# The bias of the values is added by VectorE, tile by tile, instead of by GpSimd, four tiles at a time

## What is computed

```
q, k, v = xn Wq' + bq, xn Wk' + bk, xn Wv' + bv
attention = softmax(q k' / 16) v                    # one head of 256 per batch
gates = softmax(xn Wg');  2 experts of 16 per token, their scores scaled to a sum of 1
y = sum over the 2 experts of  score * (silu(xn Gate_e') * (xn Up_e')) Down_e'
ffn = y + sigmoid(xn Wsg') * (silu(xn Ws_gate') * (xn Ws_up')) Ws_down'
```

## Time and profile before

| | us |
|---|---|
| median of 3 executions | 563.72 |
| lowest, highest | 562.06, 564.19 |
| the profiled execution | 562.47 |
| its span, first to last instruction | 560.7 |

### The profile page before, as it was taken

The page is one execution under the profiler, slowest core; times in us unless marked ns, Lnnn a source line. Parts: engine busy times, 40 slices in busy tenths (PEclk is TensorE's granted clock), DMA queues, the critical chain, the costliest instruction groups (busy, mean ns, idle before and its releaser), DMA issues.

```text
span 560.7 us, 9991 instructions
## 1 busy us (share of the span) xinstructions
PE 520.9 (93%) x3469; PEld 473.2 (84%) x3469; DVE 396.4 (71%) x806; ACT 280.4 (50%) x467; POOL 191.4 (34%) x170
## 2 busy tenths in 40 slices
PE   3999998899997899989886999999999999999997
PEld 3888987778887789988876988798989898989897
DVE  5778456998985456454453627899696969697986
ACT  3767764355643255444342544836272727272742
POOL 0001010411005666788885043244142323323410
PEclk9999999999998899999998999999999999999999
DMA  8826254302023455674447471062116111112111
GB/s 314 338 104 243 114 226 179 113 30 85 0 85 95 140 167 161 196 255 146 150 147 127 119 251 37 24 223 61 53 57 206 58 56 49 57 55 69 39 57 57
DMA packets 29888, 69.29 MB, mean 124 GB/s; under 512 B 5008, under 2 KB 9488, under 8 KB 28816
## 3 DMA queue, kind: packets, MB, share of 16 engines
q1 hardware_dynamic: 22496, 49.68, 24.7%
q0 software_dynamic: 6912, 18.88, 12.9%
q10 hardware_dynamic: 432, 0.09, 0.1%
HBM read 41.37 MB, written 27.26 MB: 122 GB/s over the span
## 4 chain that ended last, share of the span: by engine, by line
PE 76%; DVE 10%; another core or an unknown queue 4%; ACT 4%; issue 3%; DMA 1%; POOL 0%; SPq 0%; ACTq 0%; DVEq 0%; POOLq 0%
PE ps L723 47%; PE ps L904 8%; PE ps L729 7%; PE ps L845 6%; PE ps L925 5%; PE ps L806 1%; DVE probs_f L1512 1%; DVE blk_xT L1204 1%; ACT probs_f L1194 1%; DMA stage_gu<-in_shared 1%; ACT blk_xT L1009 1%; PE ps L815 1%; DMA blk_x<-rows,row 1%; DVE acc L1294 1%
## 5 line engine op out<-in xcount | busy, mean ns | idle before, releaser
L710 POOL DMA_INDIRECT rows_y<-ytab,slot x64 | 75.5, 1180 | 136.5 <-DVE acc L1528 120.1
L682 POOL DMA_INDIRECT blk_x<-rows,row x80 | 82.1, 1026 | 70.2 <-DVE row L1399 31.5
L723 PE MATMUL ps<-vv,pT 128*128 128x258 f32 x768 | 96.7, 284 | 0.0
L723 PE MATMUL ps<-xT,shared_w 128*128 128x512 f32 x384 | 94.3, 400 | 1.4 <-DVE sil L1280 1.4
L723 PEld LDWEIGHTS ps<-vv,pT 128*128 128x128 f32 x768 | 94.2, 189 | 0.5
L723 PEld LDWEIGHTS ps<-xT,shared_w 128*128 128x128 f32 x384 | 72.3, 192 | 16.8 <-issue 2.1
L723 PE MATMUL ps<-qT,xbT_hi 128*128 128x512 f32 x256 | 79.5, 392 | 1.0 <-ACT scored_t L1009 0.8
L904 PE MATMUL ps<-expert_w,blk_xT 128*128 x480 | 68.3, 292 | 6.6 <-DVE blk_xT L1204 6.4
L904 PEld LDWEIGHTS ps<-expert_w,blk_xT 128*128 128x128 f32 x480 | 61.1, 193 | 8.8 <-issue 8.4
L723 PEld LDWEIGHTS ps<-qT,xbT_hi 128*128 128x128 f32 x256 | 47.2, 188 | 11.9 <-ACT scored_t L1009 2.0
L668 POOL TENSOR_TENSOR expert_w<-stage_e,expert_w 128x768 fp32r<-128x768 f32 x7 | 13.6, 1941 | 115.2 <-ACT expert_w L1009 115.2
(11 more groups left out here) (159 smaller groups left out, 869.3 us busy)
## 6 DMA issues: line engine op xcount, KB each, us to landing
ytab<-blk_y SPq DMA_DIRECT2D x40, 256.0 KB
keys<-xT SPq DMA_DIRECT2D x8, 1024.0 KB, 5.7
stage_e<-in_experts SPq DMA_DIRECT2D x16, 384.0 KB, 3.1
rows<-xn SPq DMA_DIRECT2D x8, 512.0 KB, 2.6
xbT_hi<-keys SPq DMA_DIRECT2D x8, 512.0 KB
xbT_lo<-keys SPq DMA_DIRECT2D x8, 512.0 KB
out<-acc SPq DMA_DIRECT2D x32, 128.0 KB
acc<-in_x SPq DMA_DIRECT2D x7, 512.0 KB, 8.8
```

Of the source, the lines that this page charges most:

```text
L682: e.indirect_dma_start(out=blk_x[:, q, n, :], out_offset=None, in_=rows, in_offset=bass.IndirectOffsetOnAxis(ap=row[:, 2 * b + n:2 * b + n ...
L710: e.indirect_dma_start(out=rows_y[:, r, k, :], out_offset=None, in_=ytab, in_offset=bass.IndirectOffsetOnAxis(ap=slot[:, k, i:i + 1], axis=0),
L723: ins = e.matmul(dst, stationary(p, k), moving(q, k), start=(n == 0), stop=(n == total - 1))
```

## The change

The eight `bias_in` steps of GpSimd become 32 of VectorE, one tile each. They stand at the end of the loop's steps b = 3 to 34, so that in VectorE's queue `bias_in` b-3 comes behind the remainder of `blk_turn` b+2 and ahead of the product `blk_h` of step b+1. GpSimd keeps only the gathers in this stage. `rows_in` waits for its own tile's addition each time, which is an instruction of the same engine.

```diff
     beside = {5: ("qkv_split", 0), ..., 9: ("mix", 0), 10: ("mix", 1),
-              11: ("mix_bias",), 13: ("keys_load", 0), **{15 + 2 * c: ("bias_in", c) for c in range(NCH)}}
+              11: ("mix_bias",), 13: ("keys_load", 0)}
     for b in range(PAIRS + 2):
...
         if b in beside:
             steps.append(beside[b])
+        if 3 <= b < 3 + TILES:
+            steps.append(("bias_in", b - 3))
...
-                elif kind == "bias_in":                       # in pool_program
-                    c = a[0]
-                    if c == 0:
-                        e.wait_ge(bias_loaded, 16)
-                        e.wait_ge(shared_added, 4 * NCH)
-                    these = acc[:, CT * c:CT * (c + 1), :]
-                    e.tensor_tensor(these, these, bvb[:, :].unsqueeze(1).to_broadcast([P, CT, D]), ALU.add).then_inc(
-                        biased, 1)
...
+                elif kind == "bias_in":                       # in vector_program
+                    i = a[0]
+                    if i == 0:
+                        e.wait_ge(bias_loaded, 16)
+                        e.wait_ge(shared_added, 4 * NCH)
+                    e.tensor_tensor(acc[:, i, :], acc[:, i, :], bvb[:, :], ALU.add).then_inc(biased, 1)
...
                     e.wait_ge(gathered[r], 16 * TOPK * (i // YR + 1))
-                    if i % CT == 0:
-                        e.wait_ge(biased, i // CT + 1)
+                    e.wait_ge(biased, i + 1)
```

## The result

| | before | after |
|---|---|---|
| median, us | 563.0 (4 runs) | 556.48 (4 runs, 555.69 to 557.34) |
| ratio, 95% interval | | 0.9885 (0.9865 to 0.9904) |
| profiled execution, us | 562.47 | 556.99 |
| its span, us | 560.7 | 555.1 |

6.5 us less by the medians, 5.6 us by the two spans; 5.6 us had been forecast. The median lies inside the range, and the gain by the spans is the forecast one, to a tenth by luck, as the account further on shows. That holds for the chip of these runs. On one of the other chips the same change was worth 14.6 us, which only one of the rivals had foreseen; the experiments come to that.

What follows compares the result with a forecast made beforehand. GpSimd's queue of gathers and additions was taken to bound the block stage. 5.9 + 0.9 - 0.5 - 0.7 = 5.6 us gained, so 556.9 us profiled and 558.1 us median; range of 8 in 10: 554.0 to 563.8 us.

Steps and rivals of the forecast that it cites:

- one of the rivals: Block stage: TensorE becomes the bound, 18 pairs at 2.8 us each, 15.5 us gained, 548 us; chance 0.07.
- GpSimd's queue bounds the block stage: Block stage with additions: GpSimd is busy 54.78 of 65.90 us and waits for nobody, despite 34% on the page.
- the difference of two paces: Block stage, 18 pairs: 3.66 us a pair with GpSimd's additions, 3.33 without; 5.9 us gained.
- The low clock and the long stop go (+0.9): TensorE's stop at 293 to 300 us and the half-speed work behind it vanish: 0.9 us gained.
- a full last round comes (-0.5): End of the gathers: the short last round may become a full one of 6.7 us; 0.5 us lost.
- VectorE's additions: 0: VectorE's queue, block stage: 32 additions of 0.34 us counted as 0 on the path; upper bound 5.4 us.
- The cover: VectorE's slack around the remainders, thought to hide an addition; without it one per round is exposed, 16 x 0.34 = 5.4 us.
- Collisions 0.7 us: Block stage: gathers starting inside a VectorE addition are delayed, some 3 of 32, 0.7 us lost; bounds 0 and 13.4 us.
- the fourth rival: Block stage: VectorE's additions wait for gathers, at most 3.4 us of it on the path, 561.5 us; chance 0.04.
- the rule that it was laid beside: Trainium skill: VectorE instructions with two SBUF inputs and GpSimd instructions reading SBUF exclude each other; additions could wait 1.01 us.
- its pace of 3.33 us a pair: Block stage before the additions begin: 10 pairs in 33.29 us, taken as the new kernel's pace for 18 pairs, 59.9 us.
- The rival of the useful breaks: Block stage: additions were stops that freed TensorE's results; without them rounds of eight gathers, gain 0 to 2 us; chance 0.16.

## Why the prediction was right, and where not

1. *GpSimd's queue bounds the block stage, in spite of its 34% of the span.* Right. The 32 additions put back on it cost 12.9 of 14.6 us; on VectorE or left out altogether they make no difference (0.9733, 0.9727). On a chip with rounds the same shows in the kernel with the additions outside the block stage (the stage 6.5 us shorter) and in the one with eight additions on VectorE (0.9885).
2. *The gain is the difference of two paces, 5.9 us.* 5.5 us: the 18 pairs took 60.4 in place of 65.9 us, a round 6.68 us as read off before the additions began. The naive sum, 8 x 2.38 = 19 us, and the pace of TensorE, 15.5, were both rightly passed over for this chip. The picture was neater than the trace: between 205.60 and 222.41 the silus of the kernel before come one by one, 2.5 to 3.8 us apart, and GpSimd's waits in these rounds are 1.1 to 1.8 us, not 1.34 to 1.72. The average pace is the same.
3. *The low clock and the long stop go (+0.9), a full last round comes (-0.5).* Their sum was 0.4; from the silu of pair 32 to the end it was 260.2 us before and 259.9 after. The clock of that part is 1.00 in place of 0.92. What each of the two was worth by itself isn't shown.
4. *VectorE's additions: 0.* Right, and safer than I argued: neither twice as many nor an addition on the run to the first remainder was felt. The cover isn't that run's slack but that a round is set by GpSimd and the release behind it.
5. *Collisions 0.7 us.* Too much. 67 gathers have a median of 1.015 us and a longest one of 1.143. Only two gathers started inside an addition. This was a near thing: 12 of the 32 additions started just 0.02 to 0.03 us behind a gather, and what they would have cost ahead of it no run shows. No addition waited for a gather (0.414 to 0.439 us each), so the fourth rival is out; the rule that it was laid beside speaks of instructions of GpSimd that read SBUF, and that a gather counts as one for its whole length no run shows.
6. *The parts that should not change.* The changed kernel came to the first silu 0.6 us earlier; this is there by 30 us of the span, far ahead of the change, and in other runs of kernels with the same first stage it goes either way (0.2 us later with twice the additions, 1.2 us earlier with eight on VectorE). Between the first silu and that of pair 14 it took 0.8 us more, nearly all of it up to pair 4 (13.87 in place of 13.11 us). There its clock was at the lower level from 187.8 to 194.6 us, 6.8 us in place of the 3.4 of before. That this is the cause is likely, not shown.

The sum of the spans: 5.5 + 0.3 + 0.6 - 0.8 = 5.6 us. That it meets the forecast to a tenth is luck: the pace gave 0.4 us less and the end 0.1 less, the collisions didn't take their 0.7, and the two unforeseen parts took 0.2. The mechanism and the size of the main term were right. By the medians the gain was 6.5 us, and the median came 1.6 us below the 558.1 of the forecast.

What the prediction didn't see is that its pace of 3.33 us a pair belongs to the chip. I used it as it stood and gave TensorE's own pace 0.07. On the chip with 552.2 us that rival holds, 14.6 us where it said 15.5, and 537.65 us lies far below the range. Nothing in one trace could have told that another chip has no rounds; but the words "I can't tell from the trace why; I only use that it repeats" marked the place, and the range stopped at 554.0 us, short of the rival's 548. The rival of the useful breaks is out: without additions GpSimd stopped by itself in every round, for 1.4 to 1.8 us from 202 us on.

## What to carry to other kernels

Look for the bound in a stage, not in the span: an engine of 34% can be a full queue in the stage that counts, and the test is whether it waits for anybody there. Where the same work runs with and without the suspected cost in one trace, the difference of the two paces forecast the gain (5.9 for 5.5 us) far better than the cost that was removed (19 us), on a chip like that of the trace; on another chip the gain was 14.6 us. Before work is moved to where an engine idles, see what its neighbour does there: GpSimd's additions were free for VectorE beside operands in PSUM and made VectorE some 5.8 us late beside operands in SBUF.

## What the runs showed of the hardware

- While GpSimd issues gathers, semaphores are raised late, in batches; TensorE's results so become usable some 0.8 us after a row of gathers ends: 6.68 us for two pairs where TensorE needs 2 x 2.80. Seven raises of TensorE within 0.38 us stand against 2.80 us for the same seven without the effect. The traces of the first result and of the second and third chip show it (kernel before at 562.9 to 563.4 us), the first chip of the experiments does not (552.2 us). Plain DMAs of another queue in place of the gathers bring 2.80 us on a chip (565.1 us) whose trace shows the effect beside its remaining gathers. Why chips differ stays open.
- A gather wasn't in the way of a VectorE addition with two operands in SBUF (0.417 us, at most 0.44, with 31 of 32 beside a gather); an addition or a splitting on GpSimd was, to its end: 0.95 us became 2.79, and a cast of 64 numbers a partition 1.99 in place of 0.18.
- The additions that GpSimd did on four tiles take 2.38 us there and 1.22 us on VectorE; on one tile 0.75 and 0.42.
